# Causal attention over a three-bank ring: the second head's additions, the maxima and the values take other steps

## The reference, cut to what matters

```python
qkv = x @ W_qkv + b_qkv
Q, K, V = ...            # 16 heads of 64
scores = jnp.einsum('bqhi,bkhi->bhqk', Q, K) / jnp.sqrt(jnp.float32(HEAD_SIZE))
scores = scores + jnp.triu(jnp.full((S, S), -10000.0), k=1)
probs = jax.nn.softmax(scores, axis=-1)
vals = jnp.einsum('bkhi,bhqk->bqhi', V, probs)
return vals.reshape(B, S, NUM_HEADS * HEAD_SIZE) @ W_out + b_out
```

## Time and profile before

| | |
|---|---|
| median of 3 runs | 4431.97 us (4431.10 to 4435.25) |
| the profiled execution | 4431.71 us, span of its trace 4429.9 us |
| TensorE busy (PE) | 3906.3 us, 88% of the span |
| VectorE busy (DVE) | 3176.9 us, 72% |
| ScalarE busy (ACT) | 2043.0 us, 46% |
| GpSimd busy (POOL) | 1110.8 us, 25% |

### The profile page before, as it was taken

How to read it: one execution, slowest core, us unless ns; L and a number is a source line. 1 busy time by engine, 2 the same in 40 slices (tenths; PEclk the granted TensorE clock), 3 DMA queues, 4 the chain that set the end, 5 groups by cost and what they waited for, 6 DMA issues and landing times. The chain is left out here.

```text
span 4429.9 us, 63827 instructions
## 1 busy us (share of the span) xinstructions
PE 3906.3 (88%) x23153; PEld 1788.0 (40%) x23153; DVE 3176.9 (72%) x6950; ACT 2043.0 (46%) x3038; POOL 1110.8 (25%) x944
## 2 busy tenths in 40 slices
PE   5999999969798779999998796848999999999866
PEld 2222222254344422222222544834444444444366
DVE  6999999736666688999996466665555555656476
ACT  2577777631154326777775311523333333333334
POOL 1000000000231110000000012744444444444466
PEclk8899999979899979999999797969999999999978
DMA  4111111120210031111112201520000000000045
GB/s 111 42 42 44 42 40 40 36 94 1 70 33 1 11 94 37 44 42 41 40 40 58 66 0 48 158 83 2 2 2 2 2 2 2 2 2 2 6 135 144
DMA packets 323362, 184.06 MB, mean 42 GB/s; under 512 B 169926, under 2 KB 283258, under 8 KB 323050
## 3 DMA queue, kind: packets, MB, share of 16 engines
q1 hardware_dynamic: 306698, 145.33, 12.3%
q0 software_dynamic: 14624, 34.37, 3.1%
q10 hardware_dynamic: 1728, 0.28, 0.0%
HBM read 109.91 MB, written 68.68 MB: 40 GB/s over the span
## 5 line engine op out<-in xcount | busy, mean ns | idle before, releaser
L724 DVE TENSOR_REDUCE ra_mh<-PS 128x1 f32<-128x512 f32 x2144 | 1342.6, 682 | 99.7 <-PE PS L597 90.9
L677 ACT ACTIVATE ra_p<-PS 128x1024 f32<-128x1024 f32 x1040 | 1012.0, 1021 | 478.0 <-PE PS L604 469.7
L597 PE MATMUL PS<-ra_k,ra_q 72*128 72x512 bf16 x2144 | 751.6, 393 | 15.3 <-DVE ra_mh L724 9.0
L604 PE MATMUL PS<-ra_q,ra_k 75*128 75x512 bf16 x2080 | 622.9, 380 | 1.7
L2203 ACT ACTIVATE ca_p<-PS 128x1024 f32<-128x1024 f32 (+3 forms) x384 | 311.1, 810 | 572.1 <-PE PS L2113 368.3
L613 PE MATMUL PS<-ra_p,ra_va 128*32 128x512 f32 x4192 | 570.1, 608 | 0.3
L2263 DVE TENSOR_REDUCE ca_mh<-PS 128x1 f32<-128x512 f32 (+3 forms) x768 | 388.4, 552 | 155.0 <-PE PS L2073 125.7
L2241 POOL TENSOR_TENSOR ca_s<-ca_s,ca_p 128x1024 f32<-128x1024 f32 (+3 forms) x256 | 414.4, 1619 | 234.5 <-ACT ca_p L2203 229.2
L597 PEld LDWEIGHTS PS<-ra_k,ra_q 72*128 72x128 bf16 x2144 | 202.0, 97 | 671.4 <-DVE ra_mh L724 503.5
L572 POOL DMA_DIRECT2D o_heads<-ra_ot x134 | 70.6, 531 | 1556.6 <-ACT ra_ot L683 1556.6
L2104 PE MATMUL PS<-ca_q,ca_k 64*128 64x512 f32 (+3 forms) x1536 | 344.2, 524 | 0.0
(11 more groups left out here) (270 smaller groups left out, 5494.6 us busy)
## 6 DMA issues: line engine op xcount, KB each, us to landing
ra_k<-k_parts SPq DMA_DIRECT2D x136, 144.0 KB
ra_q<-q_parts SPq DMA_DIRECT2D x136, 144.0 KB
o_heads<-ra_ot POOLq DMA_DIRECT2D x134, 128.0 KB, 2.8
ao_ot<-o_heads SPq DMA_DIRECT2D x16, 1024.0 KB, 6.3
f_xg<-expert_tokens SPq DMA_DIRECT2D x56, 256.0 KB, 4.7
expert_outputs<-f_yb SPq DMA_DIRECT2D x56, 256.0 KB, 2.3
expert_tokens<-X SPq DMA_DIRECT2D x28, 256.0 KB
q_parts<-rp_parts SPq DMA_DIRECT2D x48, 128.0 KB, 2.4
```

The source lines that it names most:

```text
L597: pe.matmul(PS[:, 5 + place % 3, :], Q[0:KMAX, u, j, t * P:(t + 1) * P], K[0:KMAX, u, j, h * BT:(h + 1) * BT], start=True, stop=True).then ...
L604: mm = pe.matmul(PS[:, j, :], K[0:KROWS, ub, j, (step % KT) * P:(step % KT + 1) * P], Q[0:KROWS, ub, j, (step // KT) * BT:(step // KT + 1) ...
L677: act.activation(PR[:, s % 2, PH * pair:PH * (pair + 1), :], PS[:, PH * pair:PH * (pair + 1), :], ACT.Exp, scale=float(DH) ** -0.5).then_i ...
L724: dve.tensor_reduce(mh[:, pair, c // HALVES, c % HALVES:c % HALVES + 1], PS[:, bank, :], AX.X, ALU.max).then_inc(s_max, 1)
```

## The change

The list RING gets another order. Nothing else in the kernel is touched.

- Each step from one to three gets one early tile, and early 3 moves to step four. Before, early 0 and early 1 stood together in step one.
- The second half of "k" goes from ahead of the weighing in step three to behind it.
- "y" of the second query half goes from the first part of step four to the second part of step nine.
- late 4 (the first of LATE[1]) stays in step six, late 5 goes to step seven ahead of the weighing, late 6 behind it, and late 7 to step eight ahead of the weighing.
- v0 goes from step nine to step eight, ahead of "m", which stays in step eight; v1 goes from step ten to step nine. Step ten has nothing left.

```diff
     RING = [
         ([("q", 0)], [("k", 0)]),
-        ([("z", 1)], [EARLY[0], EARLY[1]]),
-        ([EARLY[2]], [("q", 1)]),
-        ([("k", 1)], [EARLY[3]]),
-        ([("y", 1)], [LATE[0][0]]),
+        ([("z", 1)], [EARLY[0]]),
+        ([EARLY[1]], [("q", 1)]),
+        ([EARLY[2]], [("k", 1)]),
+        ([EARLY[3]], [LATE[0][0]]),
         ([LATE[0][1]], [("z", 0), LATE[0][2]]),
-        ([LATE[0][3]], [LATE[1][0], LATE[1][1]]),
-        ([LATE[1][2]], [LATE[1][3]]),
-        ([], [("m", 0)]),
-        ([("v", 0)], []),
-        ([("v", 1)], []),
+        ([LATE[0][3]], [LATE[1][0]]),
+        ([LATE[1][1]], [LATE[1][2]]),
+        ([LATE[1][3]], [("v", 0), ("m", 0)]),
+        ([("v", 1)], [("y", 1)]),
+        ([], []),
         ([("y", 0)], []),
     ]
```

## The result

The changed kernel takes **4358.4 us** (median of 4 runs, 4354.3 to 4364.6) against 4432.9: a ratio of 0.983, 95% interval 0.982 to 0.985, so 74 us less. Five more runs gave 4355.4, ratio 0.984 (0.982 to 0.986). The profiled execution took 4364.6 us, span 4362.8. Every kernel of this study, the one before included, spreads over 10 to 15 us, because the stages ahead, which nobody touched, end earlier or later: the first scores of this stage start at 3001.0 in this trace and at 2991.0 in that of the five further runs, whose span is 4352.8. From there to the end both last 1361.8 us; the kernel before lasts 1431.1 (4429.9 less 2998.8), 69.3 more.

The account below looks back on a forecast made before the run. TensorE was taken as the bound, idle about 6% on ring banks VectorE had not read. Removing 0.57 + 0.57 + 0.40 + 0.46 = 2.00 us per iteration, 60.5 us together, gave 4371 us, range 4356 to 4396.

Parts of the forecast that it names:

- A: Step one: early 1 waits for a ring bank right behind early 0; 0.57 us per iteration, forecast to go.
- C: Step five: late 1 waits because late 0 is read behind the additions; 0.46 us per iteration, forecast to go.
- D: Step six: late 4 and late 5 together wait like the early pair; 0.57 us per iteration, forecast to go.
- B: Step four: late 0 waits for a bank the additions' first half holds; forecast to go only partly, gaining 0.40 us.
- Late 1 and late 4: Late maxima products forecast to fit without waiting, with 0.03 and 0.1 us to spare.
- Rival 1: Late maxima too tight: waits of 0.2 to 0.3 us each, total 4383 to 4390; chance 0.13.
- rival 5: Early 3 does not hold late 0: a further 0.6 us per iteration gained, 4352; chance 0.03.
- The additions' place: Steps nine to eleven: VectorE needs 2.46 us, TensorE leaves 3.02, so no wait and no cost.
- The cast: Maxima's path on VectorE: forecast to fall after GpSimd's add and shrink from 1.70 to under 0.4 us, at no cost.
- rival 2: The cast stays long, transfers late by up to 0.65 us: up to 20 us, 4371 to 4391; chance 0.10.
- Rivals 3 and 4: Cast behind step nine's add: about 4429, chance 0.07; behind adds of steps nine and ten: 4507, chance 0.05.
- 5.76 and 5.1: Time in us from the maxima transfers' start to their need: before the change, and after it if the cast stays 1.70.

Follow-up runs that it names:

- e1: Only early 0 and early 1 set apart, against the kernel before: 4417.0 us, ratio 0.997.
- e3: Only the second head's additions moved from step four to step nine, against the kernel before: 4386.5 us, ratio 0.990.
- e5: Changed kernel with early 2 back in step two and early 3 back in step three: 4346.6 us, ratio 0.981 to the kernel before.
- e7: Changed kernel with the second head's additions in step ten ahead of the weighing, not step nine behind it: 4368.4 us (one run).
- e6: Changed kernel with the maxima's transposition moved from step eight to behind the weighing of step nine: 4403.1 us (one run).
- e8: e5 with blocks of one shape together (queries with keys, both value blocks with the maxima): 4330.7 us, ratio 0.977 to the kernel before.
- e2: Only late 4 and late 5 set apart, late 7 moved to step eight, values left in place, against the kernel before: 4437.9 us, ratio 1.001.
- e4: Changed kernel with the maxima ahead of the values again, values in steps nine and ten: 4385.6 us, ratio 0.989 to the kernel before.

## Why the prediction was right

It said 4371 (4356 to 4396), faster with 0.88. Measured are 4358 and 4355: the range holds the first and misses the second by less than a microsecond, and both lie just below 4360, the lower end of the span to which the text gave 0.62. The sum had 60.5 where the traces show 70.4 from iteration 1 on, so it was some 10 us short. The mechanism was the forecast one, by its steps (lengths are from start to start, means over the 30 turns):

- **A**: 0.57 by the sum, 0.59 in e1; in the changed kernel the blocks from early 0 to the scores of step four, early 3 left out, take 5.45 for 6.07, so 0.62. **C**: 0.46 by the sum, 0.47 in the trace (1.76 less 1.29). **D**: 0.57 by the sum; from late 4 to the value block the changed kernel takes 5.51, where the kernel before takes 6.11 to the same point, so 0.60.
- **B** goes by less than half, and the wait that takes its place is where it was forecast: late 0 starts 1.29 after early 3 (1.30 by the sum), idle 0.45. That late 0 starts 0.89 after the weighing, not the sum's 0.99, gains nothing: the text took early 3's block as 0.31, as it is ahead of scores, and ahead of a weighing it takes 0.40. In all B gives 0.42 where the sum had 0.40. e3 and e5 show both ends of it: alone the additions' move removes B in full, and early 3 back in step three removes the rest, 0.50.
- **Late 1 and late 4** fit in their narrow margins. Late 1 follows late 0 by the unhindered 1.29, and the waits view has one kind of ring wait left. Rival 1 did not occur, and neither did rival 5: early 3 does hold late 0.
- **The additions' place** cost nothing; e7 shows how near its end was: one step later the sum 2.46 was met by 2.44, with 0.13 of wait.
- **The ends of the stage** were small, but not as told. The sum had 0.5 gained in iteration 0; in the traces it lasts 1.1 longer (40.52 for 39.41), which goes with the clock at its start, and from step two on it takes the same (27.48 and 27.49), as A falls into step one, and D against late 0 was forecast to give nothing. Behind the first scores of iteration 31 the changed kernel is 0.8 shorter, where the sum had 0.
- **The cast** got short: 0.21, no longer under an add. Here the shared ports of the Trainium skill (SBUF — State Buffer, "SBUF: two separate sides") agree with three placements: 1.70, 0.64 and 0.21 us for one and the same cast, the first two ending 0.07 to 0.08 after GpSimd's add in every turn of every trace that has them. The two operations ahead of the cast, which read PSUM, start under the same add and take 0.28 each with no hold, so it is not that the add slows all of VectorE. But it was worth next to nothing in time. The need is 5.2 us in most turns (e6), and with a cast of 1.7 the transfers would still have had 5.5 to the product (6.98 less 1.49). Seven of the 31 turns of e6 need more than that, 2.6 us in all, so I estimate the price of rival 2 at some 3 us for the whole run, not the text's up to 20: its 5.76 and 5.1 are counted to the weight load, and the product comes 0.4 later. Rivals 3 and 4 did not occur, since no add stood in the cast's place; the cast started 0.16 behind the end of the one ahead (3423.43 to 3423.59).

Two steps of the text were short, in opposite ways. The first is a term that the sum put at nothing: "the work of TensorE itself stays 37.65 less the waits" does not hold. Beyond the waits, the stretch from the value block to the next turn (3421.18 to 3430.17, 8.99) takes 0.20 less than its blocks did before (8.19 and the additions' 1.00): the value block ahead of the transposition takes 0.99 for 1.09, and the scores of step ten behind a projection 0.72 for 0.83. In the timelines, before and after (the value block before is that of 3448.29, its scores those of 3447.46; the value block after stands in the path of the maxima above):

```profile
3449.38 0.87 PE L2127 MATMUL PS<-ca_p,ca_v 128*64 128x384 f32 x4
...
3425.56 1.16 PE L2090 MATMUL PS<-ca_wo,ca_ot 64*128 64x128 f32 x16
3426.56 0.60 PE L2104 MATMUL PS<-ca_q,ca_k 64*128 64x256 f32 x4
...
3427.28 0.87 PE L2127 MATMUL PS<-ca_p,ca_v 128*64 128x384 f32 x4
```

Those are blocks without any idle time, whose length goes with their neighbour. e8 shows this as a lever of its own. The Trainium skill (TensorEngine Tiling (Array Packing), "Key Properties") says that changing the tiling mode drains TensorE; the trace agrees in kind, with 0.1 us for such a place and 0.2 for each merger, but the rule as a count of changes gives neither e7's last 0.1 nor whether a place costs 0.1 or 0.2. With this the turn is accounted for: A 0.62, B 0.42, C 0.47, D 0.60 and these 0.20 are 2.31, of the measured 2.32. Of the 0.32 that the sum lacked, 0.20 is this term and 0.11 the four waits' sizes.

The second is a cover that was not named. The text took the values ahead of the maxima as a risk to be priced, at nothing. It is more: with late 7 moved to step eight, the transposition would have waited 0.7 for late 7's maxima, and the value block hides that. e2 shows the move of the late maxima without it (no gain at all, 4438), and e4 the changed kernel without it (+0.84). The sum was right on D because both edits come together. As far as the text's reasons go that is luck: with the late maxima's move alone D would not have counted. The values' move alone was not run.

## What to carry to other kernels

In a ring of buffers, the time of a fill depends on who reads the buffer three places back: put a block of other work between two fills whose readers are slow, and take the longest reader (here 2.3 us of additions) to where other work separates it from the next fill. When a producer moves later, follow its result to the next thing that is issued in order, since the gain may be taken back there, and look for independent work to put into that hole. Once no wait is left, look at the lengths of blocks by neighbour: here, the same matmuls took 0.2 us less when a block of their own shape stood beside them.

## What the runs showed of the hardware that was not expected

Six transfers of 2 KB from SyncE take some 0.65 to 0.7 us each to issue (4.1 together) and reach TensorE's product in most turns 5.2 us after the first one's start, and 5.3 at the stage's start (3002.00 to 3007.28). In e6 seven of 31 such trains took 0.4 to 1.0 longer, so a margin of some tenths over the usual time is not enough for all turns. A bf16 cast of 16 by 128 elements on VectorE, from SBUF to SBUF, takes 0.21 us, and up to 1.70 when a GpSimd add of 2.35 us is under way; operations of the same size that read PSUM keep their 0.28 under the same add. TensorE's granted clock from the first to the second scores of the stage was 0.89 or 0.69 in traces of one and the same kernel, and the stretch lasted 8.1 or 10.7 us with it: compare stretches behind it. And blocks of matmuls without idle time differ by 0.1 us with the shape of what stands beside them; which of the neighbours' properties counts, these runs don't separate.
